# One order of steps for the second and third stage of a Perceiver layer: scans whose product stays in PSUM, scatters placed between the blocks, and closing steps in another order

## What is computed

```python
x = x + cross_attention(layernorm(x), ctx)          # 16 heads, 257 context keys and 32 own keys
x = x + time_mix(layernorm(x), ...)                 # below
x = x + mixture_of_experts(layernorm(x), ...)       # 8 experts, the best 2 of each token, and one shared

def time_mix(x):
    xx = shifted(x) - x                             # shifted by one token, zero ahead of the first
    t5 = tanh((x + xx * tmx) @ maa_w1)              # five parts of 32
    xw, xk, xv, xr, xg = (x + xx * (tm[f] + t5[f] @ maa_w2[f]) for f in range(5))
    r, k, v, g = xr @ Wr, xk @ Wk, xv @ Wv, silu(xg @ Wg)
    decay = exp(-exp(tdecay + tanh(xw @ td_w1) @ td_w2))
    def step(S, inp):                               # for each token of a sequence, S is 8 x 8 a head
        kv = k_t[:, None] * v_t[None, :]
        y = r_t @ (S + u * kv)
        return decay_t * S + kv, y
    y = scan(step)
    return (groupnorm(y) * g) @ Wo

def mixture_of_experts(x):
    top_v, top_i = top_k(x @ gate_w, 2)
    routed = the sum over both of softmax(top_v) * expert[top_i](x)   # silu(x @ Wg) * (x @ Wu) @ Wd
    return routed + silu(x @ Sg) * (x @ Su) @ Sd                      # the shared expert
```

## Time and profile before

| | |
|---|---|
| three timed runs | 632.24, 627.86, 627.23 us, median 627.86 |
| the profiled execution | 628.2 us, of which the span from the first to the last instruction is 626.5 |
| attention | 0 to about 270.5 us of the span |
| second program | about 270.5 to 518.9 |
| third program | 518.9 to 626.5 |
| busy in the span | PE 82%, VectorE 72%, ScalarE 56%, GpSimd 55% |
| granted clock of TensorE, mean | 0.903 |

### The profile page before, as it was taken

The page is one execution under the profiler, slowest core; times in us unless marked ns, Lnnn a source line. Parts: engine busy times, 40 slices in busy tenths (PEclk is TensorE's granted clock), DMA queues, the critical chain, the costliest instruction groups (busy, mean ns, idle before and its releaser), DMA issues. The chain is left out here.

```text
span 626.5 us, 14786 instructions
## 1 busy us (share of the span) xinstructions
PE 514.3 (82%) x4326; PEld 346.5 (55%) x4326; DVE 449.5 (72%) x912; ACT 349.4 (56%) x1033; POOL 345.8 (55%) x692
## 2 busy tenths in 40 slices
PE   3889999999999999825889797787644786999980
PEld 2567777777777777621223233233312666999970
DVE  7468787887878878596886795896983653666643
ACT  3678888888888888416302615306108433665540
POOL 4146666666666666437548283496690750444440
PEclk9989999999999999966789897889867776999995
DMA  9125563222222221079990000000000111222217
GB/s 216 52 62 160 171 167 91 78 67 78 72 75 75 68 81 44 11 140 163 200 141 0 0 2 0 4 13 19 9 21 5 35 36 38 65 66 65 65 35 205
DMA packets 80265, 45.34 MB, mean 72 GB/s; under 512 B 4762, under 2 KB 79092, under 8 KB 80228
## 3 DMA queue, kind: packets, MB, share of 16 engines
q1 hardware_dynamic: 77956, 40.20, 28.3%
q0 software_dynamic: 2272, 4.69, 2.2%
HBM read 29.09 MB, written 15.78 MB: 72 GB/s over the span
## 5 line engine op out<-in xcount | busy, mean ns | idle before, releaser
L578 ACT ACTIVATE probs<-psum,neg_max 128x289 f32<-128x289 f32 x256 | 126.0, 499 | 34.4 <-DVE neg_max L751 34.4
L751 DVE TENSOR_REDUCE neg_max<-psum 128x1 f32<-128x289 f32 (+1 forms) x192 | 95.4, 552 | 45.5 <-PE psum L684 45.5
L634 PE MATMUL psum<-ident,probs 128*128 128x128 f32 x512 | 83.0, 285 | 1.6 <-ACT probs L578 1.3
L634 PEld LDWEIGHTS psum<-ident,probs 128*128 128x128 f32 x512 | 59.4, 152 | 26.8 <-issue 24.7
L1612 POOL DMA_INDIRECT y_rows<-x_sq,dest_row x39 | 37.4, 958 | 54.2 <-DVE dest_row L1718 49.7
L1054 POOL TENSOR_TENSOR w_up<-recep,w_gate 128x496 f32<-128x496 f32 x32 | 42.2, 1320 | 40.3 <-DVE w_gate L1412 40.2
L469 POOL TENSOR_TENSOR inv_spread<-quad_of,inv_sum 128x128 f32<-128x128 f32 x64 | 25.6, 400 | 56.3 <-DVE inv_sum L747 56.3
L1412 DVE TENSOR_TENSOR_SCAN w_gate<-decay,w_gate 128x512 f32<-128x512 f32 x32 | 55.8, 1742 | 1.1
L578 ACT ACTIVATION_READ_ACCUMULATOR probs<-psum,neg_max 128x1 f32 x256 | 50.6, 198 | 0.0
L684 PE MATMUL psum<-kT,q_heads 32*128 32x289 f32 x512 | 49.8, 458 | 0.9 <-ACT probs L578 0.9
L1078 POOL DMA_INDIRECT x_rows<-rows_out,slot_no x32 | 41.2, 1287 | 14.1 <-issue 14.1
(11 more groups left out here) (262 smaller groups left out, 1246.0 us busy)
## 6 DMA issues: line engine op xcount, KB each, us to landing
x_rows<-blank SPq DMA_DIRECT2D x1, 9815.0 KB, 57.7
k_in<-in_ctx SPq DMA_DIRECT2D x64, 128.0 KB, 2.5
v_in<-in_ctx SPq DMA_DIRECT2D x64, 128.0 KB, 2.5
xs<-x_rows SPq DMA_DIRECT2D x39, 65.0 KB, 1.9
w_gate<-in_L_ffn_Wg SPq DMA_DIRECT2D x1, 1408.0 KB, 7.9
w_up<-in_L_ffn_Wu SPq DMA_DIRECT2D x1, 1408.0 KB, 6.8
x_res<-in_x SPq DMA_DIRECT2D x4, 256.0 KB, 4.1
v_own<-in_ctx SPq DMA_DIRECT2D x2, 512.0 KB, 7.5
```

The lines of the kernel that those rows point to most:

```text
L578: last = nc.scalar.activation(probs_of(par, gr), bank[S_BANK[gr]][:, 0:KEYS], ACT.Exp, bias=neg_max[:, par, gr:gr + 1], accum_out=row_sum[ ...
L634: last = pe.transpose(bank[PT_BANK[h]][:, P * (2 * k + c):P * (2 * k + c) + P], probs_of(par, 2 * h + k)[:, P * c:P * c + P], ident[:])
L751: nc.vector.tensor_reduce(neg_max[:, par, start:end], psum[:, start:end, 0:KEYS], AX.X, ALU.max, negate=True).then_inc(s_max, 1)
```

## The change

1. The product of a state is written back into its PSUM bank and the scan reads it there; the tensor `kv` is gone. A `PROD` bank is free after the scan (s_state) instead of after the product.
2. The first column of the difference (L1365) moves from VectorE to ScalarE (`first_diff`), with a semaphore of its own, and its place is ("shift", 0) or ("bonus_in", n-1).
3. TensorE gets filler products into a bank that nobody reads (`keep_busy`) around the transposes of the layer norm, and one ahead of the first mix product.
4. The scatters of block 0 numbered 4 to 7 move out of the loop of block 2 to the head of block 3, those of block 1 numbered 6 and 7 to behind the loop of block 3.
5. In the loop of block 3 the closing steps of block 2 from "output" on come one state earlier, and most of the shared expert of block 0 and the low part of block 1 come in from behind the loop. The first piece pair of the shared expert uses the two `MIX` banks alone.
6. "gated" of blocks 2 and 3 is done by VectorE. "turned" is cut into three steps, "top" into two halves, "shared_up" into a TensorE step and a ScalarE step. "centre" squares ahead of copying.
7. Behind the loop of block 3 the steps are in another order.

```diff
+            def sh_gate(q):
+                return bank[SH_GATE[q % 2 if q >= 2 else 0]]
+
+            def sh_up_bank(q):
+                return bank[SH_UP[q % 2] if q >= 2 else SH_GATE[1]]
...
+                if r == 1:
+                    order += [("scatter", 0, k) for k in range(4, TOP * TPB)]
...
+                    if r == 0 and 2 <= j < 6:
+                        order.append(("scatter", r, j - 2))
+                    if r == 1 and 2 <= j:
+                        order.append(("scatter", r, j - 2))
...
+                def first_diff(n):
+                    act.wait_ge(s_ln_T, NB + n + 1)
+                    if n:
+                        act.wait_ge(s_mix_out, 5 * n)
+                    nc.scalar.activation(diff[:].rearrange(SEQ, n=N)[:, :, 0:1],
+                                         ln_T[:, BLK * n:BLK * n + BLK].rearrange(SEQ, n=N)[:, :, 0:1],
+                                         ACT.Copy, scale=-1.0).then_inc(s_diff_first, 1)
...
                         act.wait_ge(s_y, D * n + D)
                         if n:
                             act.wait_ge(s_y_norm, n)
-                        nc.scalar.copy(y_cen[:], Y).then_inc(s_y_cen, 1)
-                        if n:
                             act.wait_ge(s_var, n)
                         nc.scalar.activation(y_sq[:], Y, ACT.Square).then_inc(s_y_sq, 1)
+                        nc.scalar.copy(y_cen[:], Y).then_inc(s_y_cen, 1)
...
+                def keep_busy(count):
+                    for _ in range(count):
+                        pe.matmul(POST, ident[:], w_gate[:].rearrange("p e i -> p (e i)")[:, 0:BLK], start=True, stop=True)
+
                 pe.wait_ge(s_time_w_in, 16 * TIME_W_DMAS)
+                pe.wait_ge(s_ffn_w_in, 16 * FFN_W_DMAS)
                 pe.transpose(bank[2][:, 0:NPAR], param_rows[:], ident[0:NPAR, 0:NPAR]).then_inc(s_params_turned, 1)
-                ln_tensor(pe, 1, (0, 1))
+                keep_busy(8)
+                for n in range(NB):
+                    ln_tensor(pe, 1, (0, 1), [n])
+                    keep_busy(1)
+                keep_busy(1)
...
-                            "bonus": (s_bonus, n + 1), "state": (s_kv, D * n + key_[-1] + 1)}[key_[0]]
+                            "bonus": (s_bonus, n + 1), "state": (s_state, D * n + key_[-1] + 1)}[key_[0]]
...
+                    if s == ("mix", 0, 0):
+                        keep_busy(1)
...
-                        nc.vector.tensor_tensor(dx[:, :, 1:N], x[:, :, 0:N - 1], x[:, :, 1:N], ALU.subtract)
-                        nc.vector.tensor_scalar(dx[:, :, 0:1], x[:, :, 0:1], -1.0, None, ALU.mult).then_inc(s_diff, 1)
+                        nc.vector.tensor_tensor(dx[:, :, 1:N], x[:, :, 0:N - 1], x[:, :, 1:N], ALU.subtract).then_inc(s_diff, 1)
                         v.wait_ge(s_diff, n + 1)
+                        v.wait_ge(s_diff_first, n + 1)
...
-                        nc.vector.tensor_tensor(kv[:, q % 2], prod_bank(s), key[:, par], ALU.mult).then_inc(s_kv, 1)
+                        nc.vector.tensor_tensor(prod_bank(s), prod_bank(s), key[:, par], ALU.mult).then_inc(s_kv, 1)
...
-                        nc.vector.tensor_tensor_scan(state[:, q % (LAG + 1)], decay[:, par], kv[:, q % 2], 0.0,
+                        nc.vector.tensor_tensor_scan(state[:, q % (LAG + 1)], decay[:, par], prod_bank(s), 0.0,
                                                      ALU.mult, ALU.add).then_inc(s_state, 1)
...
+                    elif s[0] == "gated" and n >= NB - 2:
+                        v.wait_ge(s_y_affine, n + 1)
+                        v.wait_ge(s_gate, n + 1)
+                        v.wait_ge(s_out, n)
+                        nc.vector.tensor_tensor(y_gated[:], y_affine[:], gate[:, par], ALU.mult).then_inc(s_y_gated, 1)
```

More of the change, by code:

```diff
@@ L945, in perceiver_layer @@
                 if r >= 0:
-                    order.append(("top", r))
+                    order += [("top", r, 0), ("top", r, 1)]
                 for j in range(D):
@@ L968, in perceiver_layer @@
             last, r = NB - 1, NB - 2
-            order += [("y", last, D - 2), ("rows", r), ("turn", r), ("shared_low", 0), ("y", last, D - 1), ("centre", last), ("turned", r),
-                      ("shared_up", 0, 0), ("variance", last), ("logits", r), ("top", r), ("shared_up", 0, 1), ("gap", r),
-                      ("norm", last), ("places", r), ("slots", r), ("shared_low", 1), ("gated", last),
-                      ("shared_hidden", 0, 0), ("shared_hidden", 0, 1), ("output", last)]
-            order += [("scatter", r, k) for k in range(5)]
@@ L974, in perceiver_layer @@
[L974 to L978 removed]
+            order += [("scatter", r - 1, k) for k in (6, 7)]
@@ new lines, in perceiver_layer @@
+            order += [("y", last, D - 2), ("rows", r), ("turn", r), ("y", last, D - 1), ("turned_T", r), ("centre", last),
+                      ("tile_list", last), ("variance", last), ("logits", r), ("top", r, 0), ("shared_down", 0), ("norm", last),
+                      ("top", r, 1), ("gated", last), ("places", r), ("turned_high", r), ("gap", r), ("turned_rows", r), ("slots", r),
+                      ("output", last)]
+            order += [("scatter", r, k) for k in range(4)]
+            order += [("ln_centre", last), ("shared_up", 1, 0), ("shared_act", 1, 0), ("ln_variance", last), ("shared_hidden", 1, 0),
+                      ("shared_up", 1, 1), ("shared_act", 1, 1), ("rows", last), ("turn", last), ("shared_hidden", 1, 1)]
```

100 lines of the change are left out of this document (59 added, 41 removed).

## The result

The changed kernel takes 606.35 us at the median of 4 runs (605.87 to 609.89) against 627.55 (625.63 to 632.24) for the kernel before. The ratio is 0.966, 95% interval 0.960 to 0.973. The last group of runs had it once more on another chip: 606.05, six runs, ratio 0.963 (0.960 to 0.966). Medians and ranges here are of all runs of a kernel, while ratios leave out runs that took over 1.5% more than its fastest. The forecast was 601, with a range of 591 to 613.

What follows compares the result with a forecast made beforehand. The prediction took VectorE's queue, with waits for GpSimd inside it, to bound the loops, and a cross-engine chain the stretch behind block 3. Gains of 1.9 + 3.7 + 7.5 + 1.5 + 12.0 = 26.6 us gave 601, range 591 to 613.

Steps and rivals of the forecast that it cites:

- The start: Ahead of the first `mix_part`: fillers hold TensorE's clock up, hidden products take 2.1 instead of 4.0 us; gain 1.9 us.
- The first column: L1365 off VectorE in the loops of blocks 0 to 2: three times 1.22 us saved, gain 3.7 us.
- The scans: Loops over states: scans from PSUM stop waiting for GpSimd; blocks 0 to 3 gain 0, 2.5, 4.0, 1.0, sum 7.5 us.
- The joints: Between the blocks: GpSimd lags less, so last y and row norm come earlier; gain 1.5 us, between 0 and 4.
- Behind the loop: After block 3's last scan: the new order reaches the last slot number in 29.0 instead of 41.0 us; gain 12.
- the scans still wait: Rival, loops over states: scans still wait for GpSimd and the 7.5 us go, giving 609; chance 0.07.
- the clock stays low: Rival, start, joints and behind the loop: TensorE's clock stays down where its queue is thin, giving 607; chance 0.15.
- The held bank: Rival, loops over states: the bank kept through the scan makes the loop a chain, 34 us lost, giving 635; chance 0.04.

Runs made afterwards that it cites:

- run 7: Changed kernel with nine casts behind the tanh, three scatters instead of four ahead of the last row root, block 1's shared down product behind the place products: 609.06 us.
- run 11: Changed kernel with the second nine casts of weights behind the tanh of block 0 and without TensorE's filler products: 605.45 us, ratio 0.964 to the kernel before.
- run 3: Changed kernel with the first column of the difference back on VectorE: 610.67 us at the median, runs from 604.64 to 614.75.
- run 1: Kernel before with only the scans reading the product out of PSUM: 615.67 us against 628.75, ratio 0.977.
- run 2: Changed kernel with its scans out of SBUF again: 618.61 us, ratio 0.983 to the kernel before.
- run 5: Changed kernel without TensorE's filler products at the start, the early wait for the feed-forward weights left in: 614.5 us.

## Why the forecast held

The time was 5 us above the forecast of 601 and well inside the range. But of the five terms one was too small, and three, 7.1 us together, brought next to nothing. That the scans' 5.6 us more made up for most of these is luck. Of the 5 us that are left, 1.9 stand ahead of the first layer norm reduce, where nothing was changed. The ends of the range aren't the sums that they are said to be: the bounds of the terms add up to 589 and 618, not 591 and 616. The measured time is inside either.

- **The start, 1.9 us: the step from the hidden products to the first `mix_part` failed.** The clock rose as predicted, and `mixed_x`, which was to end when it did, ended 1.4 us earlier behind the first reduce. So the hidden products end 3.2 us earlier. But the row of 3.55 us of idle time was read as a wait for TensorE alone. Between the product and the `mix_part` stands the tanh, and ahead of it on ScalarE 18 casts. Before, the tanh had waited 0.98 us for the product, so a us was all that the casts left to win, and they now begin 15.2 us behind the first reduce instead of 14.4. The first `mix_part` gained 0.2 us and the first product of a state lost 0.4 (42.0 against 41.6). The term comes back, at 1.8 to 2.5, once the tanh is moved (runs 7 and 11).
- **The first column, 3.7 us: failed.** The prediction itself called L1365's 1.22 us a wait for GpSimd, and yet counted it as gone with the instruction. The next pass with two SBUF inputs takes it over: 0.2 us in all four loops (run 3).
- **The scans, 7.5 us: right in mechanism, mis-sized.** The term is net of the passes that come into block 3, charged 3.4 and 1.2 = 4.6 there. Without them its own numbers give 12.1 for the scans alone, and run 1 measured 13.1, run 2 12.3. Net, the four loops gave 13.4, of which the column has 0.2. Block 3 came as forecast, 1.1 against 1.0: the loop would have been 22.1 and is 26.4, so what moved in cost 4.3. Block 1 gave 2.6 against 2.5, though only 0.7 in run 1. Too small were block 2, 6.2 against 4.0, and block 0, 3.4 against nothing. Block 0 was held to be TensorE's by its busy time, and that time counts records at the lower level at their full length.
- **The joints, 1.5 us:** nothing, 34.1 before and 34.0 after. At the third, `ln_var` is now held to 1.9 us, until GpSimd's `read` ends, and `rows_out` to 1.8, since GpSimd's `mixed` follows the row root at once.
- **Behind the loop, 12.0 us: right, 10.9.** Of its milestones `gated` came at 12.7 (predicted ahead of the 14.0 for `output`), the root at 19.7 (19.2), the logits' end at 25.1 (24), the last slot number at 30.1 (29.0). Part of the last us is the down product of 3.76 us ahead of the place products (run 7 got 0.5 back).
- **The rivals.** That the scans still wait is out. That the clock stays low cost nothing in the profiled execution, and is seen in other runs: the loop of block 1 with the same code took 27.1, 28.7 and 32.7 us at mean clocks of 1.00, 0.94 and 0.79. The held bank turned nothing into a chain; VectorE's idle time ahead of all 32 products is 6.3 us, against 9.4 before.

The Trainium skill, "VectorE: DVE Perf Modes", section on the TRN2 errata, would have made the 32 scans 2.1 us longer out of PSUM, an estimate from its fixed parts of 120 and 58 cycles. They take 1220 ns there against 1224 at the shortest from SBUF, so the trace doesn't bear out that difference.

What stays open is why TensorE's clock differs between executions in the loop of block 1, whose code is the same in most of these kernels; it is worth up to 5.6 us, and was not tried. In all four loops it comes to 7.8 us (run 5). Block 2 took 27.5 or 30.1 us with the same code at a mean clock of 0.94 both times, so the mean clock isn't all of it.

## What to carry to other kernels

An instruction that is long because it waits for another engine can't be moved away with its wait: look for the next one in the queue that needs the same thing, and change what it needs (here one input in PSUM) rather than where it runs. When a wait ends with an engine's result, walk back through every queue on the way, also those that are idle by their sums; casts ahead of one tanh cost 3.0 to 3.7 us and hid what the clock and the earlier `mixed_x` had gained. And a gain at a milestone is only one when the next stage waits for that milestone: the slot numbers came 0.5 us earlier in run 7, and the stretch behind them was 3.6 us longer.

## What the runs showed of the hardware

What waits for GpSimd on VectorE is narrower than "reads SBUF". Two more lines of the changed kernel, in ns, are those of `norm` and `ln_var`:

```profile
L1469 DVE TENSOR_TENSOR x_cen<-x_sq x4: 666/680/1740, 355.7 to 462.6; 128x512 f32<-128x512 f32 x4
L1498 DVE TENSOR_SCALAR ln_var<-ln_sqsum x4: 169/746/1904, 374.2 to 471.3; 128x4 f32<-128x4 f32 x4
```

Scans and products with one input in PSUM never do (64 instructions, spread under 30 ns). Passes with two SBUF inputs do when a read of GpSimd's is under way (`mixed_x` 0.75 or 1.62, `norm` 0.67 or 1.74). So does a scalar operation with a single SBUF input and 4 or 16 elements a partition (`ln_var` 0.17 to 1.90, the column 1.23). A reduction over 512 elements out of SBUF doesn't (0.66 to 0.69 always, L1486). The Trainium skill, "SBUF — State Buffer", section "Who interferes with whom", states the same split: two SBUF inputs and the forms that can take both ports contend with GpSimd, one input outside them and reductions don't. The trace agrees in these rows; that the small scalar operations took both ports is not shown by any.
